# Feature attention with its mixing cut in two between heads, ten early maxima, and key casts one tile ahead

## The chip, the cores and the metric

The kernel runs on one core of a Trainium2 chip. Its engines run their own instruction queues in order and meet at semaphores: TensorE (PE: matmul, and PEld its weight load), VectorE (DVE), ScalarE (ACT), GpSimd (POOL), SyncE (SP, which issues the DMAs). The metric is the device time of one execution in microseconds (us), lower is better.

## The reference

A decoder of two layers over x (32 x 64 rows of 256) and a context of the same size, in fp32. Two of its six parts are touched: the first (differential attention) at its end, and the second, which is the feature attention below. It attends between the 256 *columns* of each batch, in 8 heads of 8 rows.

```
x = x + differential_attention(layernorm(x))
x = x + feature_attention(layernorm(x), ctx, ctx, W)

def feature_attention(q, k, v, W):            # q, k, v: (32, 64, 256)
    qh, kh, vh = (a.reshape(32, 8, 8, 256) for a in (q, k, v))
    a = einsum('bhdq,bhdk->bhqk', qh, kh) * 8 ** -0.5
    p = softmax(a, axis=-1)                    # 256 x 256 for each of 32 x 8
    y = einsum('bhqk,bhdk->bhdq', p, vh).reshape(32, 64, 256)
    return selu(einsum('oc,bct->bot', W, y))
```

## The kernel before

The 2048 rows are 16 tiles of 128 rows (two batches, b = 0 and 1). Queries and keys are split into bf16 parts and stacked in DRAM and back (`q_stack`, `k_stack`, lanes of 64 partitions), so that a bf16 matmul of 48 rows gives fp32 products.

The feature attention runs in *turns*, t = -1 to 16, and in turn t each engine works on several tiles. For every head h of every batch b of tile t+1, PE computes the scores (`largest`, L1015, two matmuls into PSUM bank h % 2) and DVE takes the row maximum (`maximum`, L842). So 16 maxima go through two banks, and PE may refill a bank only after DVE has read it (`max_taken`). Beside each `largest` PE computes the scores of tile t (`score`, L1020), with the maxima of the turn before as three further rows of the query stack. ACT turns each pair of heads into exponentials (`exponentials`, L901, 128 x 1024). `mix(tile, slot, b, half)` (L1032) multiplies the exponentials of four heads by the values, eight matmuls of 32 columns. These are the four *mixes* of a turn; I write "mix 0.1" for batch 0, half 1, and "head 0.3" for batch 0, head 3.

What follows a mix: ACT copies the result (`take_mixed`, L905, once for each batch), PE transposes it (`turn_mixed`, L1040), DVE divides by the sums (`divide`, L853 and L856), PE transposes both batches (L1093), ACT copies (`mixed_c`, L918), PE multiplies by W (`w_out`, L1101), ACT and POOL make the selu (L927 to L938, L998 to L1004) and add it to x.

How the maxima reach the queries: when 8 of them are taken, POOL splits them into three bf16 parts (`split_max`, four instructions, L980 to L986), PE transposes them (`turn_max`, L1047), ACT copies them (`max_to_rows`, L895) and SP writes them with two DMAs into the query stack (`max_to_stack`, L806). The heads of that batch in the next stage wait for the landing (`max_stacked`).

The order of the work is written out by hand for each engine. On PE a turn is eight calls `heads(b, g)`, each two heads with nothing between them, with the other work between these calls:

```
heads(0,0) mix(t-1) 1.1, turn_max(t,1)     heads(0,1) turn_mixed(t-1,1)
heads(0,2) transposes of mixed             heads(0,3) mix 0.0
heads(1,0) w_out                           heads(1,1) mix 0.1, turn_max(t+1,0)
heads(1,2) turn_mixed(t,0), context        heads(1,3) mix 1.0
```

The differential attention before it is also a pipeline in turns, t = -3 to 16, bound by PE except at its end. Turns 15 and 16 drain it: PE transposes probabilities (L629), multiplies by values (L672), transposes `scaled` (L683) and `headsT` (L690), multiplies by the output weights (L696); DVE sums squares (L553), scales (L563), divides and subtracts (L569 to L576) and adds to x (L579). Its last turns also carry the casts and splits of the context into `k_parts` (ACT L478, POOL L361 to L365).

## Time and profile before

| | us |
|---|---|
| median of 3 runs | 1336.93 |
| lowest, highest | 1335.71, 1339.19 |
| profiled execution, its own time | 1332.79 |
| its span from first to last instruction | 1330.7 |
| PE busy, DVE busy, ACT busy | 1215.3, 958.9, 709.2 |
| feature attention, about | 212 to 450 |

The profiled execution lies 4.1 us under the median. The timeline view gives, for each instruction or run of like instructions, its start, its length, the engine and line, what it writes and reads, how many, and in brackets how long the engine was idle before it and what released it.

### The profile page before, as it was taken

The numbers are of one execution on the slowest core, as the hardware profiler recorded it, in microseconds if no ns is written. First come the engines' busy times: TensorE is split into PE (matmuls) and PEld (weight loads), VectorE is DVE, ScalarE is ACT, GpSimd is POOL, SyncE is SP. The second block draws the span as 40 slices with busy tenths as digits, with TensorE's granted clock in tenths as the row PEclk, the third lists the DMA queues.
The fourth block names the chain that finished last, engine by engine and source line by source line (L and its number), as shares of the span: only waits on it lengthen the run. The fifth ranks groups of instructions, "written<-read, shape, count | busy, mean of one in ns | idle before, by whom it ended". The sixth has DMA issues, their size and how long they took to land. (4 is left out here: it accounts for less than half of the span.)

```text
span 1330.7 us, 27523 instructions
## 1 busy us (share of the span) xinstructions
PE 1215.3 (91%) x9976; PEld 963.9 (72%) x9976; DVE 958.9 (72%) x1862; ACT 709.2 (53%) x1475; POOL 454.5 (34%) x537
## 2 busy tenths in 40 slices
PE   4999988988888779798899999999997999999998
PEld 3677764444444557697677878788786899999998
DVE  5899986888887376887567778677775668555555
ACT  2778763777778546000466565656653463333332
POOL 1444642354553224565552423323240301112210
PEclk8999997999999988899999999999999999999999
DMA  5111161133231210000400000000000300000001
GB/s 173 36 36 37 46 147 32 41 80 95 77 94 35 55 60 0 1 0 13 135 9 4 4 8 4 8 4 8 4 1 9 87 25 25 25 25 25 1 1 64
DMA packets 58660, 51.04 MB, mean 38 GB/s; under 512 B 9064, under 2 KB 50888, under 8 KB 58184
## 3 DMA queue, kind: packets, MB, share of 16 engines
q1 hardware_dynamic: 58574, 49.88, 13.4%
q8 instruction: 56, 0.92, 0.3%
q14 instruction: 30, 0.25, 0.1%
HBM read 37.93 MB, written 11.53 MB: 37 GB/s over the span
## 5 line engine op out<-in xcount | busy, mean ns | idle before, releaser
L842 DVE TENSOR_REDUCE fa_neg_max<-psum 128x2 f32<-128x512 f32 x256 | 163.6, 685 | 35.6 <-PE psum L1015 34.7
L901 ACT ACTIVATE fa_probs<-psum 128x1024 f32<-128x1024 f32 x128 | 130.3, 1020 | 45.5 <-PE psum L1020 44.9
L1872 PE MATMUL psum<-mo_xT_high,mo_w_high 128*128 128x256 f32 x512 | 145.2, 284 | 3.0 <-DVE mo_xT_low L2706 2.8
L1872 PE MATMUL psum<-mo_xT_low,mo_w_high 128*128 128x256 f32 x512 | 144.9, 283 | 0.0
L1872 PE MATMUL psum<-mo_xT_high,mo_w_low 128*128 128x256 f32 x512 | 144.2, 282 | 0.0
L2538 ACT ACTIVATE mo_silu<-psum 128x256 f32<-128x256 f32 x128 | 49.0, 384 | 155.0 <-PE psum L1872 155.0
L2672 DVE TENSOR_TENSOR mo_mid<-mo_silu,psum 128x256 f32<-128x256 f32 x128 | 53.6, 419 | 92.8 <-ACT mo_silu L2538 92.7
L1015 PE MATMUL psum<-stacks_k_stack,stacks_q_stack 48*128 48x256 bf16 x512 | 93.5, 287 | 16.7 <-DVE fa_neg_max L842 7.7
L2008 POOL TENSOR_TENSOR ga_probs<-ga_probs,ga_top 128x1024 f32<-128x1024 f32 x16 | 30.5, 1905 | 203.6 <-DVE ga_top L2162 203.6
L1872 PEld LDWEIGHTS psum<-mo_xT_high,mo_w_high 128*128 128x128 f32 x512 | 97.0, 189 | 3.4 <-DVE mo_xT_low L2706 3.0
L1872 PEld LDWEIGHTS psum<-mo_xT_low,mo_w_high 128*128 128x128 f32 x512 | 97.2, 190 | 0.0
L1872 PEld LDWEIGHTS psum<-mo_xT_high,mo_w_low 128*128 128x128 f32 x512 | 97.0, 189 | 0.0
L2479 POOL TENSOR_TENSOR mo_w_low<-mo_raw,mo_w_high 128x512 fp32r<-128x512 f32 x21 | 27.6, 1315 | 188.0 <-ACT mo_w_high L2513 188.0
L1020 PE MATMUL psum<-stacks_q_stack,stacks_k_stack 51*128 51x256 bf16 x512 | 87.4, 280 | 0.2 <-DMA stacks_q_stack<-fa_max_rows 0.2
L1015 PEld LDWEIGHTS psum<-stacks_k_stack,stacks_q_stack 48*128 48x128 bf16 x512 | 33.0, 96 | 72.4 <-DVE fa_neg_max L842 42.2
L1997 POOL TENSOR_TENSOR ga_q_scaled<-ga_q,ga_q_inv 128x1024 f32<-128x1024 f32 x32 | 70.1, 2190 | 38.0 <-ACT ga_q_inv L2039 38.0
L2032 ACT ACTIVATE ga_q_scaled<-ga_q 128x512 f32<-128x512 f32 x64 | 40.3, 632 | 61.8 <-DVE ga_q L2135 61.8
L1032 PE MATMUL psum<-fa_probs,fa_values 128*32 128x256 f32 x1024 | 70.0, 392 | 2.5 <-ACT fa_probs L901 0.4
L1872 PE MATMUL psum<-mo_w_high,mo_mid_high 128*128 128x256 f32 x256 | 72.3, 282 | 0.0
L1872 PE MATMUL psum<-mo_w_low,mo_mid_high 128*128 128x256 f32 x256 | 71.9, 281 | 0.0
L1872 PE MATMUL psum<-mo_w_high,mo_mid_low 128*128 128x256 f32 x256 | 71.7, 280 | 0.0
L2335 PE MATMUL psum<-ga_w_o_high,ga_mixedT_high 128*128 128x256 f32 x256 | 63.0, 287 | 4.9 <-DVE ga_mixedT_low L2154 4.9
(434 smaller groups left out, 3548.0 us busy)
## 6 DMA issues: line engine op xcount, KB each, us to landing
k_parts<-da_k_parts SPq DMA_DIRECT2D x96, 64.0 KB, 2.0
stacks_k_stack<-k_parts SPq DMA_DIRECT2D x32, 192.0 KB
q_parts<-stacks_parts SPq DMA_DIRECT2D x48, 64.0 KB, 2.0
stacks_q_stack<-q_parts SPq DMA_DIRECT2D x32, 96.0 KB
x<-in_x SPq DMA_DIRECT2D x4, 512.0 KB, 7.7
da_context<-in_ctx SPq DMA_DIRECT2D x4, 512.0 KB, 7.9
stacks_q_stack<-q_parts SPq DMA_DIRECT2D x32, 64.0 KB
fa_context<-in_ctx SPq DMA_DIRECT2D x16, 128.0 KB, 2.2
```

What stands on the lines that cost most here:

```text
L842: nc.vector.tensor_reduce(neg_max[:, b, :, head_at(h)], ps[:, h % 2, :].rearrange("p (q k) -> p q k", q=2), AX.X, ALU.max, negate=True).th ...
L901: nc.scalar.activation(probs[:, g].rearrange("p h k q -> p h (k q)"), ps[:, 2 + 2 * (g % 2):4 + 2 * (g % 2), :], ACT.Exp).then_inc(exp_don ...
L1015: return nc.tensor.matmul(ps[:, h % 2, q * E:(q + 1) * E], q_stack[lane, slot, b, h // LANES, q * P:(q + 1) * P], k_stack[lane, slot, b, h ...
L1020: return nc.tensor.matmul(ps[:, 2 + h % 4, k * E:(k + 1) * E], k_stack[lane, slot, b, h // LANES, k * P:(k + 1) * P], q_stack[lane, slot, ...
L1032: done = nc.tensor.matmul(ps[32 * c:32 * c + 32, 6, half * E:(half + 1) * E], values[:, slot, k, 8 * b + head_at(h), :], probs[:, h // 2, ...
L1872: done = nc.tensor.matmul(out, lhsT[i], rhs[j], start=start and k == 0, stop=stop and k == 2)
L1997: nc.gpsimd.tensor_tensor(q_scaled[:, columns].rearrange("p (h d) -> p h d", d=G_HD), q[:, columns].rearrange("p (h d) -> p h d", d=G_HD), ...
L2008: nc.gpsimd.tensor_tensor(probs[:], probs[:], top[:, :, None].to_broadcast([P, G_HEADS, SEQ]), ALU.subtract).then_inc(shifted, 1)
L2032: nc.scalar.activation(q_scaled[:, g * G_CHUNK:(g + 1) * G_CHUNK], q[:, g * G_CHUNK:(g + 1) * G_CHUNK], ACT.Square).then_inc(squares_ready, 1)
L2335: nc.tensor.matmul(ps[:, 6, 0:E], mixedT_high[:, h], weight[:, h], start=(h == 0 and weight is w_o_high), stop=False)
L2538: nc.scalar.activation(silu[:, j % 4], ps[:, j % 4, 0:2 * P], ACT.Silu).then_inc(silu_ready, 1)
L2672: nc.vector.tensor_tensor(mid[:, j % 4], silu[:, j % 4], ps[:, j % 4, 2 * P:4 * P], ALU.mult).then_inc(mid_ready, 1)
```

## The change

Four things are changed.

1. **Mixing in halves.** `mix` gets an argument k and issues only four of its eight matmuls. Each half stands after a single head: `heads(b, g)` becomes `head(b, h)`. The first half waits as the mix did, the second waits for nothing, and `mixed_done` comes with the second. Around it, `w_out` moves from after `heads(1,0)` to after head 1.3 and also waits for `max_rows_ready` of the next tile; `turn_max(t+1, 0)` no longer waits for `channels_read`; `divide(t-1, 1)` moves two heads later on DVE.
2. **ACT and POOL orders.** `take_mixed(t, 0)` and `max_to_rows(t+1, 0)` stand ahead of `exponentials(t, 1, 1)`. POOL adds the selu one turn later, and splits the maxima ahead of the queries and of clearing the values.
3. **Ten early maxima.** Of tile 0's 16 maxima, ten are scored and taken in turns 15 and 16 of the differential attention, through banks 4 and 5. The stack of tile 0 gets a semaphore of its own.
4. **Key casts.** ACT casts the context of tile t+2 instead of tile t+1 in a turn; the last split waits for `values_ready`.

```diff
+    def take_maximum(self, core, bank, b, h):
+        return core.nc.vector.tensor_reduce(self.neg_max[:, b, :, head_at(h)], core.psum[:, bank, :].rearrange("p (q k) -> p q k", q=2),
+                                            AX.X, ALU.max, negate=True)
...
+                stacks.load_q(sp, n, n, stacked if n else first_stacked)
+                stacks.load_k(sp, n, n, stacked if n else first_stacked)
...
+                    if valid(t) and not valid(t + 2):
+                        pool.wait_ge(values_ready, t + 1)
                     split_keys(t + 1)
...
+                if at(t, -1):
+                    act.wait_ge(context_loaded[0], 16)
                     nc.scalar.copy(k_parts[:, t + 1, 0], context[:, t + 1]).then_inc(k_highs, 1)
+                    for group in context_loaded[1:]:
+                        act.wait_ge(group, 16)
+                if started(t, -1) and valid(t + 2):
+                    nc.scalar.copy(k_parts[:, t + 2, 0], context[:, t + 2]).then_inc(k_highs, 1)
...
+            def early_maxima(first, last):
+                for n in range(first, last):
+                    dve.wait_ge(early_scored, n + 1)
+                    stacks.take_maximum(core, 4 + n % 2, n // C_HEADS, n % C_HEADS).then_inc(early_taken, 1)
...
+                if at(t, TILES - 1):
+                    early_maxima(0, 3)
+                if at(t, TILES):
+                    early_maxima(6, 7)
...
+                if at(t, TILES - 1):
+                    early_maxima(3, 6)
+                if at(t, TILES):
+                    early_maxima(7, EARLY_MAXIMA)
...
+            def early_scores(first, last):
+                if first == 0:
+                    pe.wait_ge(first_stacked, 16 * (LANES + LANES * PARTS))
+                    pe.wait_ge(shifted[1], TILES)
+                    pe.wait_ge(ones_loaded, 16 * LANES)
+                for n in range(first, last):
+                    if n >= 2:
+                        pe.wait_ge(early_taken, n - 1)
+                    for q in range(2):
+                        done = stacks.largest(core, 4 + n % 2, 0, n // C_HEADS, n % C_HEADS, q)
+                    done.then_inc(early_scored, 1)
...
+                if at(t, TILES - 1):
+                    early_scores(0, 2)
...
+                if at(t, TILES - 1):
+                    early_scores(2, 4)
...
                     if at(t, TILES):
+                        early_scores(6, 8)
...
+                if at(t, TILES):
+                    early_scores(8, EARLY_MAXIMA)
...
+                if at(t, TILES - 1):
+                    early_scores(4, 6)
...
+            dve.sem_inc(max_taken, EARLY_MAXIMA)
+
             def maximum(tile, b, h):
+                if isinstance(tile, int) and 16 * tile + 8 * b + h < EARLY_MAXIMA:
+                    return
                 dve.wait_ge(max_scored, 16 * tile + (8 * b + h + 1))
-                nc.vector.tensor_reduce(neg_max[:, b, :, head_at(h)], ps[:, h % 2, :].rearrange("p (q k) -> p q k", q=2),
-                                        AX.X, ALU.max, negate=True).then_inc(max_taken, 1)
+                stacks.take_maximum(core, h % 2, b, h).then_inc(max_taken, 1)
...
-                        if g == 1 and b == 0 and valid(t - 1):
+                        if g == 2 and b == 0 and valid(t - 1):
                             divide(t - 1, 1)
-                        if g == 2 and b == 0 and valid(t - 2):
+                        if g == 0 and b == 1 and valid(t - 2):
                             row_stats(t - 2)
                         if g == 2 and b == 1 and valid(t):
                             divide(t, 0)
...
                     exponentials(t, 0, 3)
-                if valid(t):
                     exponentials(t, 1, 0)
+                    take_mixed(t, 0)
+                if valid(t + 1):
+                    max_to_rows(t + 1, 0)
+                if valid(t):
+                    exponentials(t, 1, 1)
                 if valid(t - 1):
                     act.wait_ge(projected, t)
                     if started(t, 2):
                         act.wait_ge(selu_sum, t - 1)
                     nc.scalar.activation(below[:], ps[:, 7, E:2 * E], ACT.Relu, scale=-1.0).then_inc(selu_parts, 1)
                     nc.scalar.activation(above[:], ps[:, 7, E:2 * E], ACT.Relu, scale=SELU_SCALE).then_inc(channels_read, 1)
...
             def turn(t, ring, rounds, valid):
+                if isinstance(t, int) and t == -1:
+                    pool.sem_inc(split_done, 1)
+                if valid(t - 2):
+                    add_selu(t - 2)
+                if valid(t + 1):
+                    split_max(t + 1, 0)
+                if isinstance(t, int) and t == -1:
+                    clear_values()
                 if valid(t + 3) and started(t, 1):
                     split(t + 3, ring(3), rounds(3))
-                if isinstance(t, int) and t == -1:
-                    pool.sem_inc(split_done, 1)
-                    clear_values()
...
                 if valid(t + 1):
                     split_max(t + 1, 1)
+                if isinstance(t, int) and t == TILES:
+                    add_selu(t - 1)
...
-            def mix(tile, slot, b, half):
-                pe.wait_ge(exp_done, 8 * tile + (4 * b + 2 * half + 2))
-                if half == 0:
-                    if b or started(tile, 1):
-                        pe.wait_ge(mixed_ready, 2 * tile + b)
-                    pe.wait_ge(values_ready, tile + 1)
-                for k in range(2):
-                    for c in range(4):
-                        h = 4 * half + c
-                        done = nc.tensor.matmul(ps[32 * c:32 * c + 32, 6, half * E:(half + 1) * E], values[:, slot, k, 8 * b + head_at(h), :],
-                                                probs[:, h // 2, h % 2, k, :], start=(k == 0), stop=(k == 1), skip_group_check=True)
-                done.then_inc(mixed_done, 1)
+            def mix(tile, slot, b, half, k):
+                if k == 0:
+                    pe.wait_ge(exp_done, 8 * tile + (4 * b + 2 * half + 2))
+                    if half == 0:
+                        if b or started(tile, 1):
+                            pe.wait_ge(mixed_ready, 2 * tile + b)
+                        pe.wait_ge(values_ready, tile + 1)
+                for c in range(4):
+                    h = 4 * half + c
+                    done = nc.tensor.matmul(ps[32 * c:32 * c + 32, 6, half * E:(half + 1) * E], values[:, slot, k, 8 * b + head_at(h), :],
+                                            probs[:, h // 2, h % 2, k, :], start=(k == 0), stop=(k == 1), skip_group_check=True)
+                if k == 1:
+                    done.then_inc(mixed_done, 1)
 
...
+                def head(b, h):
...
-                heads(0, 0)
+                head(0, 0)
                 if valid(t - 1):
-                    mix(t - 1, ring(-1), 1, 1)
+                    mix(t - 1, ring(-1), 1, 0, 1)
+                head(0, 1)
+                if valid(t - 1):
+                    mix(t - 1, ring(-1), 1, 1, 0)
+                head(0, 2)
+                if valid(t - 1):
+                    mix(t - 1, ring(-1), 1, 1, 1)
                 if valid(t):
                     pe.wait_ge(values_ready, t + 1)
                     turn_max(t, 1)
...
-                heads(0, 3)
-                if valid(t):
-                    mix(t, ring(0), 0, 0)
-                heads(1, 0)
-                if valid(t - 1):
-                    pe.wait_ge(mixed_c_ready, t)
-                    nc.tensor.matmul(ps[:, 7, E:2 * E], w_out[:], mixed_c[:], start=True, stop=True).then_inc(projected, 1)
-                heads(1, 1)
-                if valid(t):
-                    mix(t, ring(0), 0, 1)
+                head(0, 7)
+                if valid(t):
+                    mix(t, ring(0), 0, 0, 0)
+                head(1, 0)
+                if valid(t):
+                    mix(t, ring(0), 0, 0, 1)
+                head(1, 1)
                 if valid(t + 1):
                     if isinstance(t, int) and t == -1:
                         pe.wait_ge(loaded, 32)
                     if valid(t - 1):
-                        pe.wait_ge(channels_read, t)
+                        pe.wait_ge(mixed_c_ready, t)
                     elif valid(t):
                         pe.wait_ge(max_rows_ready, 2 * t + 2)
                     turn_max(t + 1, 0)
-                heads(1, 2)
+                if valid(t):
+                    mix(t, ring(0), 0, 1, 0)
+                head(1, 2)
+                if valid(t):
+                    mix(t, ring(0), 0, 1, 1)
+                head(1, 3)
+                if valid(t - 1):
+                    pe.wait_ge(mixed_c_ready, t)
+                    if valid(t + 1):
+                        pe.wait_ge(max_rows_ready, 2 * t + 3)
+                    nc.tensor.matmul(ps[:, 7, E:2 * E], w_out[:], mixed_c[:], start=True, stop=True).then_inc(projected, 1)
+                head(1, 4)
                 if valid(t):
                     turn_mixed(t, 0)
+                head(1, 5)
+                head(1, 6)
...
+                    if valid(t - 1):
+                        pe.wait_ge(channels_read, t)
...
-                heads(1, 3)
-                if valid(t):
-                    mix(t, ring(0), 1, 0)
+                head(1, 7)
+                if valid(t):
+                    mix(t, ring(0), 1, 0, 0)
```

What now stands in a row on PE in a steady turn of the feature attention, from the middle of batch 0's heads to the middle of batch 1's. L1015 and L1020 (before), L204 and L1074 (after) are `largest` and `score`, L1032 and L1086 the mixing, L1101 and L1182 `w_out`, L1047 and L1102 `turn_max`; "..." stands for further rows of heads alone. Before:

```order
L1093 MATMUL psum<-ident,fa_mixed 128x128 x2
...
L1032 MATMUL psum<-fa_probs,fa_values 32x256 x8
L1015 MATMUL psum<-stacks_k_stack,stacks_q_stack 128x256
L1020 MATMUL psum<-stacks_q_stack,stacks_k_stack 128x256
...
L1101 MATMUL psum<-fa_mixed_c,fa_w_out 128x256
...
L1032 MATMUL psum<-fa_probs,fa_values 32x256 x8
L1047 MATMUL psum<-fa_ident_bf,fa_max_parts 24x128 x2
```

After:

```order
L1155 MATMUL psum<-ident,fa_mixed 128x128 x2
...
L1086 MATMUL psum<-fa_probs,fa_values 32x256 x4
L204 MATMUL psum<-stacks_k_stack,stacks_q_stack 128x256
L1074 MATMUL psum<-stacks_q_stack,stacks_k_stack 128x256
...
L1102 MATMUL psum<-fa_ident_bf,fa_max_parts 24x128 x2
L1086 MATMUL psum<-fa_probs,fa_values 32x256 x4
...
L1182 MATMUL psum<-fa_mixed_c,fa_w_out 128x256
```

Each block of eight is now two blocks of four with one head between them, `turn_max` stands ahead of both halves of mix 0.1 and `w_out` behind them.

ACT in the same turn, from the copy `mixed_c` (L918, after L971) on; L901 and L954 are the exponentials, L905 and L958 `take_mixed`, L895 and L948 `max_to_rows`, L927/L928 and L984/L985 the two selu parts. Before:

```order
L918 COPY fa_mixed_c<-psum 128x256
L901 ACTIVATE fa_probs<-psum 128x1024 x2
L927 ACTIVATE fa_below<-psum 128x256
L928 ACTIVATE fa_above<-psum 128x256
L901 ACTIVATE fa_probs<-psum 128x1024
L905 COPY fa_mixedT<-psum 128x512
L895 CAST fa_max_rows<-psum 24x256
L938 ACTIVATE fa_exp_below<-fa_below 128x256
```

After:

```order
L971 COPY fa_mixed_c<-psum 128x256
L954 ACTIVATE fa_probs<-psum 128x1024 x2
L958 COPY fa_mixedT<-psum 128x512
L948 CAST fa_max_rows<-psum 24x256
L954 ACTIVATE fa_probs<-psum 128x1024
L984 ACTIVATE fa_below<-psum 128x256
L985 ACTIVATE fa_above<-psum 128x256
L989 ACTIVATE fa_exp_below<-fa_below 128x256
```

The copy and the cast moved ahead of one exponential and of the selu parts, which follow `w_out`.

DVE in turn 15 of the differential attention and the start of turn 16. Before:

```order
L553 TENSOR_REDUCE da_square_sum<-da_squares 128x16
L563 TENSOR_TENSOR da_scaled<-da_attn,da_rms_inv 128x256
L569 RECIPROCAL da_inv<-psum 128x32
L571 TENSOR_TENSOR da_part<-psum,da_inv 128x256
```

After:

```order
L573 TENSOR_REDUCE da_square_sum<-da_squares 128x16
L208 TENSOR_REDUCE stacks_neg_max<-psum 128x2 x3
L587 TENSOR_TENSOR da_scaled<-da_attn,da_rms_inv 128x256
L208 TENSOR_REDUCE stacks_neg_max<-psum 128x2 x3
L597 RECIPROCAL da_inv<-psum 128x32
L599 TENSOR_TENSOR da_part<-psum,da_inv 128x256
```

Three maxima (L208) stand ahead of `scaled` and three ahead of the reciprocal. PE at the same place, before:

```order
L672 MATMUL psum<-da_probsT,da_values 64x2x64 x16
L683 MATMUL psum<-ident,da_scaled 128x128 x2
L690 MATMUL psum<-ident,da_headsT 128x128 x8
L696 MATMUL psum<-da_w_o,da_attnT 128x256 x2
```

After:

```order
L715 MATMUL psum<-da_probsT,da_values 64x2x64 x16
L204 MATMUL psum<-stacks_k_stack,stacks_q_stack 128x256 x4
L729 MATMUL psum<-ident,da_scaled 128x128 x2
L738 MATMUL psum<-ident,da_headsT 128x128 x8
L204 MATMUL psum<-stacks_k_stack,stacks_q_stack 128x256 x4
L746 MATMUL psum<-da_w_o,da_attnT 128x256 x2
```

The scores of maxima 2 and 3 stand behind the product with the values, those of 4 and 5 behind the transposes of `headsT`; those of 0 and 1 stand further up.

## Rows read from the trace of the kernel before

**Rows 1.** Windows of the whole core, us: start:end length, engines, clock, DMA share

```profile
200.00:206.00 6.00, 5.72 (x63) 5.13 (x62) 2.26 (x6) 3.15 (x8) 0.61 (x2) 1.00 0.26 66
...
216.00:222.00 6.00, 5.43 (x20) 1.14 (x18) 5.59 (x11) 0.36 (x1) 1.42 (x6) 0.50 0.01 2
...
340.00:360.00 20.00, 17.92 (x216) 8.23 (x218) 17.17 (x33) 15.75 (x25) 8.95 (x22) 1.00 0.38 98
```

**Rows 2.** Group of instructions, 212 to 440 us: busy, mean ns, idle before

```profile
L842 DVE TENSOR_REDUCE fa_neg_max<-psum 128x2 f32<-128x512 f32 x256 | 163.6, 685 | 35.6 <-PE psum L1015 34.7
```

**Rows 3.** Timeline, one steady turn: start, length, instruction, idle before it

```profile
267.95 0.27 PE L1015 MATMUL psum<-stacks_k_stack,stacks_q_stack 48*128 48x256 bf16 x1 [0.44 <-DMA stacks_q_stack<-fa_max_rows]
...
268.37 1.29 DVE L842 TENSOR_REDUCE fa_neg_max<-psum 128x2 f32<-128x512 f32 x2 [0.82 <-PE psum L1015]
...
272.11 0.41 PE L1093 MATMUL psum<-ident,fa_mixed 128*128 128x128 f32 x2 [0.18 <-DVE fa_mixed L856]
...
273.21 0.28 PE L1015 MATMUL psum<-stacks_k_stack,stacks_q_stack 48*128 48x256 bf16 x1 [0.20 <-DVE fa_neg_max L842]
...
273.54 1.07 PE L1032 MATMUL psum<-fa_probs,fa_values 128*32 128x256 f32 x16
...
274.54 0.28 PE L1015 MATMUL psum<-stacks_k_stack,stacks_q_stack 48*128 48x256 bf16 x1
...
274.75 0.22 POOL L980 TENSOR_TENSOR fa_max_parts<-fa_neg_max,stacks_zeros 128x16 bf16<-128x16 f32 x1 [1.68 <-DVE fa_neg_max L842]
...
274.96 2.48 DVE L842 TENSOR_REDUCE fa_neg_max<-psum 128x2 f32<-128x512 f32 x4 [0.29 <-PE psum L1015]
...
275.08 0.70 PE L1101 MATMUL psum<-fa_mixed_c,fa_w_out 128*128 128x256 f32 x2
...
275.65 0.22 POOL L986 TENSOR_TENSOR fa_max_parts<-fa_max_rest,fa_max_parts 128x16 bf16<-128x16 f32 x1
...
276.63 1.07 PE L1032 MATMUL psum<-fa_probs,fa_values 128*32 128x256 f32 x16
...
277.52 0.28 PE L1047 MATMUL psum<-fa_ident_bf,fa_max_parts 128*24 128x128 bf16 x2
...
277.77 0.59 ACT L905 COPY fa_mixedT<-psum 128x512 f32<-128x512 f32 x1
...
278.16 1.29 DVE L842 TENSOR_REDUCE fa_neg_max<-psum 128x2 f32<-128x512 f32 x2 [0.71 <-PE psum L1015]
278.25 0.36 ACT L895 CAST fa_max_rows<-psum 24x256 bf16<-24x256 f32 x1
```

**Rows 4.** Timeline of DVE and PE: starts of turn 1 and turn 15

```profile
240.92 0.28 PE L1015 MATMUL psum<-stacks_k_stack,stacks_q_stack 48*128 48x256 bf16 x1
...
431.61 0.40 PE L1020 MATMUL psum<-stacks_q_stack,stacks_k_stack 51*128 51x256 bf16 x4 [0.19 <-DMA stacks_q_stack<-fa_max_rows]
```

**Rows 5.** Timeline, last two turns of the differential attention

```profile
200.76 1.97 PE L672 MATMUL psum<-da_probsT,da_values 128*64 128x128 f32 x32 [0.28 <-POOL da_values L388]
...
201.63 0.42 DVE L563 TENSOR_TENSOR da_scaled<-da_attn,da_rms_inv 128x256 f32<-128x256 f32 x1 [2.18 <-ACT da_rms_inv L451]
...
204.10 0.36 DVE L569 RECIPROCAL da_inv<-psum 128x32 f32<-128x32 f32 x1 [2.04 <-PE psum L690]
...
210.50 0.43 DVE L581 BATCH_NORM_STATS2 row_stats<-x 128x6 f32<-128x256 f32 x1
```

**Rows 6.** Timeline, start of the feature attention

```profile
213.73 8.26 DVE L842 TENSOR_REDUCE fa_neg_max<-psum 128x2 f32<-128x512 f32 x12 [1.17 <-PE psum L1015]
...
225.01 0.37 PE L1015 MATMUL psum<-stacks_k_stack,stacks_q_stack 48*128 48x256 bf16 x1 [0.37 <-DMA stacks_q_stack<-fa_max_rows]
```

**Rows 7.** Page, DMA issues: count, KB each, us from issue to landing

```profile
fa_context<-in_ctx SPq DMA_DIRECT2D x16, 128.0 KB, 2.2
```

**Rows 8.** Timeline, last turns of the feature attention

```profile
437.08 0.40 PE L1020 MATMUL psum<-stacks_q_stack,stacks_k_stack 51*128 51x256 bf16 x4
...
441.92 1.93 PE L1032 MATMUL psum<-fa_probs,fa_values 128*32 128x256 f32 x32 [0.39 <-ACT fa_probs L901]
```

96 lines of the change are left out of this document (44 added, 52 removed).

## The prediction

> **What bounds the kernel now.** I read the windows first: the feature attention runs at the full clock from about 238 us on, with PE busy 17.92 and DVE 17.17 of 20 us, so neither engine has much to spare and neither is full [rows 1]. The groups then say what DVE waits for: its 256 maxima take 163.6 us and it stands idle 35.6 us before them, nearly all on PE's scores [rows 2]. The timeline says where. Turn 1 starts at 240.92 and turn 15 at 431.61 [rows 4], so 14 steady turns take 190.7 us, 13.62 each. In one such turn [rows 3] DVE idles 0.82 us at the start, 0.29 after mix 0.0 and 0.71 after mix 0.1 with `turn_max`. The first of these is no mixing: PE's head 0.0 waits there 0.44 us for the DMA that carries the maxima. So two loops hold a turn at 13.6 us, the two PSUM banks between PE and DVE, and a chain mix 0.1, `take_mixed`, `max_to_rows`, DMA, head 0.0 of the next turn. The change touches both. What to see in these rows: the 16 matmul instructions of mix 0.0 cost DVE only 0.29 us as they stand.
>
> **The prices for a steady turn**, all from [rows 3], clock 1.00:
> - A maximum follows the last after 0.60 us (four in 2.48) and lasts 0.68. DVE starts 0.42 after PE starts a head (274.54 to 274.96), and PE starts the head two further on about 0.06 after the maximum that frees its bank.
> - The second head of a pair to the mix: 273.21 to 273.54, 0.33. A mix to the next head: 273.54 to 274.54, 1.00. To `turn_max` it is 0.89. Two mixes in a row, in turn 16, take 1.93 against 1.07 for one [rows 8], so eight matmuls take 0.86 and 0.14 is lost once for each block. Half a mix then is 0.43 + 0.14 = 0.57 to the next head.
> - A head alone, with no other kind behind it, is 0.23. So a head with half a mix is 0.33 + 0.57 = 0.90 on PE, against 0.60 on DVE.
> - `take_mixed` starts 1.14 after its mix (276.63 to 277.77), so 0.71 after a last half; the cast for the rows ends 0.84 later (278.61). The four POOL instructions of `split_max` take 1.12 (274.75 to 275.87). From the rows (278.61) to the head that needs them, the next head 0.0 at 267.95 + 13.6 = 281.55, it is 2.95.
>
> **Mixing in halves.** PE's own work rises. Four more blocks are entered and left, at 0.10 (0.33 less 0.23) and 0.14: 1.0 us a turn. Before the change an estimate by these prices for all of PE's blocks is 11 us of 13.6, and 12 after, of a turn that I now walk. Times are from PE's start of head 0.0.
> Half mix, 0.1 at 0.90, half mix, 0.2 at 1.80, half mix and `turn_max(t,1)` at 2.6, 0.3 at 2.8, 0.4 at 3.0. The copy of batch 1 can start only 0.71 after its last half, at 2.8, so `turn_mixed` comes at 3.5 and 0.5 at 4.0. Head 0.6 waits for an exponential and a bank until 4.7. DVE divides after head 0.5, to 5.6, and the transposes of `mixed` start at 5.75 (before at 272.11, which is 4.16). Head 0.7 at 6.1, half mix, 1.0 at 7.0, half mix, 1.1 at 7.9. Before, 1.0 stands at 6.6. Then a stall: maximum 0.7 ends at 7.2, POOL has split it at 8.35, and `turn_max(t+1,0)`, which came 2.8 us after the POOL start, now stands at 8.2 and waits to 8.5. Half of mix 0.1, 1.2 at 9.3, second half at 9.6, 1.3 at 10.2. `take_mixed` starts at 10.3 and the rows are there at 11.15 (before at 10.66, which is 278.61). **The new wait:** `w_out` now needs these rows. PE is through with head 1.3 at 10.5 and stands 0.7 us to 11.25; behind it in PE's queue is every head of the rest of the turn, and DVE waits for them. Head 1.4 comes at 11.8 (before 9.8), `turn_mixed` at 12.1, 1.5 at 12.6. DVE takes maximum 1.5 from 13.0 to 13.7 and divides to 14.2, so 1.7 is on PE at 13.8, the last half mix at 14.3 and the next head 0.0 at 14.9, where the bank is free too. The DMA landed at 14.15 and is no longer the last. The same walk with the old order gives every start of [rows 3] to within some 0.1 us and 13.6 for the turn, which is why I trust it.
> The walk gives 14.9 us, 1.3 more a turn. Two prices no row shows. The second half waits for no semaphore, so the way into it may be short of 0.33: bounded by 0.22 (back to back with the head's 0.23) and 0.33. And a half might lose less than 0.14 (at least 0: 0.43) or more (at most the fill of a whole block, 0.64). With the low ends throughout, 0.25 + 0.43, the walk still gives 14.1, because the POOL stall grows and the wait for the rows stays; with the high ones 15.4. I take the upper middle, 14.8, nearest to the rows measured: +1.2 x 14 = **+16.8 us** (+7 to +25).
> Here a rule of the skill bears on the price. [Rows 3] show 0.10 into and 0.14 out of a block of mixing, between heads on 64-row lanes and a mix on 32-column strips. The Trainium skill, page "TensorEngine Tiling (Array Packing)", section "Key Properties", says that changing the tiling mode, not just the tile, drains the engine; by that rule four more blocks pay both ends, as summed above, and without it the low end (14.1) would hold.
>
> **Last turns.** Turn 15 has no maxima. PE's first halves again stand ahead of `turn_max(15,1)`: rows at 3.6 and head 1.0 at 6.6 after its start, where the profile has 437.08 less 431.61, 5.5 [rows 4, 8]. From head 1.0 on the copy for batch 0 now stands ahead of exponential 1.1 and the selu parts ahead of 1.2, so the last exponential ends some 1.4 later than now. Together **+2.5** (bounds +1 and +3).
>
> **Turn 0** runs at half clock before and, I take it, after. The same walk with doubled PE prices gives 15.3 us against 15.9 (225.01 to 240.92 [rows 4, 6]): **-0.6** (-2 to +1).
>
> **Early maxima, in the drain** [rows 5]. Maxima 0 and 1 fit behind `square_sum` while DVE waits 2.18 us for the root. But DVE's queue has maximum 2 ahead of `scaled`, and its score stands on PE behind the product with the values, which starts at 200.76 and ends at 202.7. DVE gets it at 203.1 and `scaled` comes at 203.7 instead of 201.63. Its transposes and those of `headsT` behind them are late by 1.5. Then maxima 4 and 5, scored behind these transposes at 205.4, run to 207.1, and the reciprocal starts at 207.0 instead of 204.10: 2.9 late. All after it is a chain (attn, squares, root, scaled, output, x); maximum 6 hides in the wait for the root, 7 to 9 behind the last transposes. The end, 210.93, is **+3.0** later (+2 to +3.5).
>
> **Early maxima, at the start of the feature attention** [rows 6]. Twelve maxima run 213.73 to 221.99 and the last of 16 ends at 225.4, PE's turn 0 starting at 225.01. After the change only six are left. They stand behind `turn_max(0,0)`, which now waits for two small loads issued at 212.4 and 212.8 (landing some 2.2 later [rows 7]), so the first starts near 215.95 on the same scale. Two maxima, 0.8 us of statistics, and four more at 0.69, with the context's transposes between the last two, end at 221.0; PE starts turn 0 at 220.4. That is **-4.6** (-6.5, if the loads are quicker, to -3).
>
> **Key casts.** ACT's cast, POOL's split of keys 15 and then the values' copy held PE 0.28 us at 200.76 [rows 5]; ACT's copy of the probabilities is ready only 0.1 before that. **-0.1** (-0.3 to +0.2). The rest of that attention is bound by PE. POOL's work is the same, only earlier.
>
> **Sum**: 16.8 + 2.5 - 0.6 + 3.0 - 4.6 - 0.1 = +17.0 us. On the profiled execution's own 1332.79 us that is 1349.8. The median of the runs lies 4.1 above it, and I put the same change on that: 1336.93 + 17.0 = 1354.
>
> **Rivals.**
> 1. *The drain of a half is cheap* (0.25 + 0.43): turns of 14.1, +7 in place of +16.8, sum +7.2, 1344. For it: the second halves wait for nothing. Against: 0.14 is lost at each block seen. Chance 0.2.
> 2. *Halves close DVE's gaps as they are placed to*, and the kernel is faster. Mechanism: if head plus half a mix fits in DVE's 0.60 us, DVE runs through from 0.0 to 1.3, and each turn loses its idle of 0.82 + 0.29 + 0.71 less the 0.7 at `w_out`: 12.5 us, -1.1 x 14 = -15.4, and with the other parts about -15, 1322. It decides at 0.60 on PE for a head with half; the rows say 0.90, and two bf16 pairs with eight passes of mixing alone are 0.23 + 0.43 = 0.66. If only half of this comes, some -5. Chance 0.1.
> 3. *No change to measure*: turns of 13.7, the early maxima's net -1.6 paying for them. It needs both low prices and `w_out` not waiting, as if mix 0.1 ended a head earlier. Chance 0.05.
> 4. *The early maxima cost more than they give*: the clock falls earlier in the longer drain or turn 0 runs at half clock throughout, +3 to +5 on top of my sum, 1358. At 216 to 222 us the granted clock is 0.50, the 1.2 GHz level, with PE waiting for DVE [rows 1]; after, PE has still less to do there. Chance 0.1.
> My own forecast has 0.55.
>
> **Chances and range.** Faster by over 0.3% (4 us, about what a measurement of this kernel can tell from no change) 0.1, within 0.05, slower 0.85. The range of 1340 to 1362 takes in rival 1, rival 4 and the bounds of the half's price; it leaves out rivals 2 and 3.
>
> **What would show it.** In the profile after: turns of 14.8 us; DVE idle 0.3 us before nearly every maximum beside a half mix, and some 0.9 after head 1.3; PE waiting 0.7 us ahead of L1182 for the cast of the rows; no more wait for the DMA at head 0.0; heads with a half between them 0.90 apart. In the drain the reciprocal of turn 15 starts 2.9 later, and 4.6 are won before turn 0. I am wrong if heads with a half between follow each other in 0.7 us or less, or if `w_out` finds the rows ready.

## The result: 1.2% slower

The changed kernel takes 1351.11 us in the median of 4 runs (1347.38 to 1355.31), the kernel before 1336.32 in the median of its 4. The ratio is 1.0124, 95% interval 1.0099 to 1.0150, so 13 to 20 us are lost, 14.8 by the medians. Forecast were 1354 and +17.

The profiled execution of after has a span of 1353.1 us, 22.4 more than that of before. It is the slowest of its four, and that of before lies below the median of its own, so the two traces lie 7.6 us further apart than the medians. The windows of the whole core, as in [rows 1] (stretch, length, busy time and count of PE, PEld, DVE, ACT, POOL, granted clock, DMA share, GB/s), with a steady stretch of the feature attention last:

```profile
216.00:222.00 6.00, 4.25 (x20) 1.34 (x20) 4.22 (x13) 1.12 (x4) 2.91 (x2) 0.50 0.26 82
...
280.00:300.00 20.00, 17.34 (x204) 6.61 (x206) 16.52 (x31) 14.37 (x22) 9.50 (x23) 1.00 0.31 75
```

and the group of the maxima, from the page, as in [rows 2] (busy time, mean ns of one, idle time before them and who ended most of it):

```profile
L208 DVE TENSOR_REDUCE stacks_neg_max<-psum 128x2 f32<-128x512 f32 x256 | 172.5, 689 | 52.0 <-PE psum L204 50.6
```

DVE now stands 52.0 us ahead of its maxima where it stood 35.6 (the new group also counts the ten early ones), and in a steady stretch PE and DVE are both less busy than they were: 17.34 and 16.52 us in 20, against 17.92 and 17.17. More waits, then, not only more work. Over the 14 steady turns PE was busy 12.07 us a turn before and 12.88 after; the idle rest went from 1.55 to 2.21. One steady turn shows them. The columns are start, length, instruction, and in brackets the idle time before it and who ended it. L208 is the maximum, L1074 `score` (the rows shown are each the first of a head), L1086 half a mixing block, L1102 the turning of maxima, L1155 the transposes of `mixed`, L1182 the product with `w_out`:

```profile
281.61 0.28 PE L1074 MATMUL psum<-stacks_q_stack,stacks_k_stack 51*128 51x256 bf16 x1
...
281.93 0.64 PE L1086 MATMUL psum<-fa_probs,fa_values 128*32 128x256 f32 x8
282.50 0.28 PE L1074 MATMUL psum<-stacks_q_stack,stacks_k_stack 51*128 51x256 bf16 x1
282.82 0.64 PE L1086 MATMUL psum<-fa_probs,fa_values 128*32 128x256 f32 x8
...
283.40 0.28 PE L1074 MATMUL psum<-stacks_q_stack,stacks_k_stack 51*128 51x256 bf16 x1
...
285.06 0.66 PE L1095 MATMUL psum<-ident,fa_mixedT 128*128 128x128 f32 x4
...
287.40 0.41 PE L1155 MATMUL psum<-ident,fa_mixed 128*128 128x128 f32 x2 [0.69 <-DVE fa_mixed L909]
...
290.21 0.22 PE L1102 MATMUL psum<-fa_ident_bf,fa_max_parts 128*24 128x128 bf16 x1 [0.28 <-POOL fa_max_parts L1037]
...
291.87 0.58 ACT L958 COPY fa_mixedT<-psum 128x512 f32<-128x512 f32 x1 [0.85 <-PE psum L1086]
...
292.35 0.36 ACT L948 CAST fa_max_rows<-psum 24x256 bf16<-24x256 f32 x1
...
292.86 0.67 PE L1182 MATMUL psum<-fa_mixed_c,fa_w_out 128*128 128x256 f32 x2 [0.73 <-ACT fa_max_rows L948]
...
296.83 0.28 PE L1074 MATMUL psum<-stacks_q_stack,stacks_k_stack 51*128 51x256 bf16 x1
```

Head 0.0 starts at 281.61, and the first three heads follow each other with half a block between them by 0.89 (282.50, 283.40). PE waits 0.69 us for DVE's division and 0.73 at the product with `w_out` for the cast of the rows at 292.35. (Between 300 and 400 us these two waits are 0.79 and 0.63 a turn.) The maxima are turned at 290.21. The next head 0.0 comes at 296.83, 15.2 us after the last. Over all, turn 1 starts at 236.42 and turn 15 at 447.68, 14 turns of 15.09 where [rows 4] gave 13.62:

```profile
236.42 0.28 PE L1074 MATMUL psum<-stacks_q_stack,stacks_k_stack 51*128 51x256 bf16 x1
...
447.68 0.39 PE L1074 MATMUL psum<-stacks_q_stack,stacks_k_stack 51*128 51x256 bf16 x2
```

**The bill, piece by piece**, each from the same instruction in both traces:

| Stretch | Before | After | Difference | Forecast |
|---|---|---|---|---|
| up to the first tile's addition to x | 52.41 | 51.25 | -1.2 | none |
| from there to tile 13's addition (key casts) | 145.85 | 145.32 | -0.5 | -0.1 |
| drain, to the last addition | 11.78 | 14.74 | +3.0 | +3.0 |
| to the first head of turn 0 | 14.97 | 10.14 | -4.8 | -4.6 |
| turn 0 | 15.91 | 14.97 | -0.9 | -0.6 |
| 14 steady turns | 190.69 | 211.26 | +20.6 | +16.8 |
| turn 15 to the last statistics of x | 19.95 | 22.20 | +2.2 | +2.5 |
| all behind the feature attention | 879.1 | 883.2 | +4.1 | none |

The last line lies in code that the change leaves alone, and so does most of the first, which moves by itself: over the twelve kernels below it stood between 50.1 and 54.4. Without both, the change costs 19.5 us in this pair of executions; the medians say 14.8, and the interval of the ratio ends at 20.

### The profile page after: what moved, and what is told of

It reads as the page before. It is cut to its first block and busy times, and to the rows that moved or that the text cites. A ratio compares the mean times of both kernels' runs of the same rounds, so it can differ in the third digit from the quotient of the medians.

```text
span 1353.1 us, 27548 instructions
## 1 busy us (share of the span) xinstructions
PE 1233.3 (91%) x9976; PEld 958.8 (71%) x9976; DVE 971.2 (72%) x1862; ACT 710.8 (53%) x1475; POOL 453.9 (34%) x537
## 5 line engine op out<-in xcount | busy, mean ns | idle before, releaser
L208 DVE TENSOR_REDUCE stacks_neg_max<-psum 128x2 f32<-128x512 f32 x256 | 172.5, 689 | 52.0 <-PE psum L204 50.6
L954 ACT ACTIVATE fa_probs<-psum 128x1024 f32<-128x1024 f32 x128 | 129.8, 1023 | 37.2 <-PE psum L1074 37.2
L204 PE MATMUL psum<-stacks_k_stack,stacks_q_stack 48*128 48x256 bf16 x512 | 97.8, 282 | 8.5 <-ACT fa_probs L954 3.3
L2082 POOL TENSOR_TENSOR ga_probs<-ga_probs,ga_top 128x1024 f32<-128x1024 f32 x16 | 30.5, 1905 | 203.7 <-DVE ga_top L2236 203.7
L1074 PE MATMUL psum<-stacks_q_stack,stacks_k_stack 51*128 51x256 bf16 x512 | 98.1, 279 | 0.3 <-ACT fa_probs L954 0.2
L204 PEld LDWEIGHTS psum<-stacks_k_stack,stacks_q_stack 48*128 48x128 bf16 x512 | 28.4, 95 | 84.8 <-issue 47.6
L1086 PE MATMUL psum<-fa_probs,fa_values 128*32 128x256 f32 x1024 | 83.1, 396 | 2.8 <-ACT fa_probs L954 0.7
```

The source lines that it names most:

```text
L204: return core.nc.tensor.matmul(core.psum[:, bank, q * E:(q + 1) * E], self.q_stack[lane, slot, b, h // LANES, q * P:(q + 1) * P], self.k_s ...
L208: return core.nc.vector.tensor_reduce(self.neg_max[:, b, :, head_at(h)], core.psum[:, bank, :].rearrange("p (q k) -> p q k", q=2), AX.X, A ...
L954: nc.scalar.activation(probs[:, g].rearrange("p h k q -> p h (k q)"), ps[:, 2 + 2 * (g % 2):4 + 2 * (g % 2), :], ACT.Exp).then_inc(exp_don ...
L1074: return nc.tensor.matmul(ps[:, 2 + h % 4, k * E:(k + 1) * E], k_stack[lane, slot, b, h // LANES, k * P:(k + 1) * P], q_stack[lane, slot, ...
L1086: done = nc.tensor.matmul(ps[32 * c:32 * c + 32, 6, half * E:(half + 1) * E], values[:, slot, k, 8 * b + head_at(h), :], probs[:, h // 2, ...
L2082: nc.gpsimd.tensor_tensor(probs[:], probs[:], top[:, :, None].to_broadcast([P, G_HEADS, SEQ]), ALU.subtract).then_inc(shifted, 1)
```

## The experiments

Each kernel was timed beside the kernel before on the same chip, but not all on one chip: "halves joined" to "halves, old order" shared one, the next four a second, the next three a third, and the last had a fourth. Ratios of different groups are compared through the kernel before. "Turn" is the mean steady turn of the profiled execution, from the cast of the rows in turn 1 to that in turn 15.

| Kernel | Ratio to before (95%) | Turn, us |
|---|---|---|
| before | 1 | 13.62 |
| after | 1.0124 (1.0099 to 1.0150) | 15.09 |
| halves joined | 1.0243 (1.0207 to 1.0278) | 15.81 |
| `w_out` later | 1.0066 (1.0042 to 1.0090) | 14.28 |
| early maxima and casts alone | 0.9976 (0.9956 to 0.9996) | 13.58 |
| halves, old order | 1.0050 (1.0019 to 1.0082) | 14.06 |
| new order, whole blocks | 1.0092 (1.0075 to 1.0109) | 14.60 |
| early maxima placed anew | 0.9944 (0.9927 to 0.9961) | 13.59 |
| two exchanges | 0.9998 (0.9972 to 1.0025) | 13.73 |
| exchanges, maxima and casts | 0.9977 (0.9964 to 0.9991) | 13.69 |
| exchanges and POOL's order | 0.9940 (0.9916 to 0.9963) | 12.98 |
| all of these | 0.9895 (0.9839 to 0.9951) | 13.00 |
| all of these, in halves | 1.0062 (1.0038 to 1.0086) | 14.30 |
| all of these, one block divided | 0.9881 (0.9856 to 0.9907) | 12.82 |

### Which part costs what: dividing, or the order

**Early maxima and casts alone.** The feature attention's orders are those of before; only the drain, the first turn and the casts are as changed.

> The changed kernel with the feature attention's old order (whole mixing blocks, w_out between heads 1.1 and 1.2, ACT, DVE and POOL as before), so the early maxima and the earlier key casts alone. From the two traces: 2.9 us lost in the drain, 4.4 won before turn 0, 0.5 from the casts, turns of 13.6 as before. Sum -2.0 us, ratio 0.9985; the drain's reciprocal again 2.9 us late. The rival, that the early maxima also hurt or help turn 0 by its clock, would show turn 0 more than 1 us off 15.9 and the sum beyond -1 to -3.

Measured: 0.9976, -3.2 us. The drain took 2.9 more than before (tile 13's addition to x at 199.60, tile 14's at 209.96), the stretch of the casts 0.5 less, and from the end of the drain to the first rows of turn 1 it was 5.4 us less. Start and turn 0 together thus gave 5.4, where I had put 4.4 for the start and nothing for turn 0. The start alone gave 5.6 here (the first head of turn 0 comes 9.40 after the last addition, 14.97 before, 10.14 in the changed kernel). The part as a whole is a small gain, and its loss in the drain is real.

**Halves in the old order.** Each second half stands where the whole block stood, each first half one head earlier:

```diff
+                if valid(t):
+                    mix(t, ring(0), 0, 0, 0)
                 head(0, 7)
                 if valid(t):
-                    mix(t, ring(0), 0, 0, 0)
                     mix(t, ring(0), 0, 0, 1)
                 head(1, 0)
                 head(1, 1)
...
```

This is one block of the four; the other three are divided in the same way.

> The early maxima and casts as changed, and the mixing in halves, but each second half where the whole block stood before and each first half one head earlier, with w_out, the turning of the maxima and the orders of ACT, DVE and POOL as before. Against the kernel with early maxima and casts alone it shows what dividing costs by itself. My theory: four more blocks at 0.24 are 1.0 us of PE; heads with a half between follow at 0.90 instead of 0.60 for DVE; turns of 14.4 (14.2 to 14.7). If the new order of w_out, ACT and POOL is worth something to the halves, as the change supposes, this one is above 15.1; if dividing is free, it stays at 13.6.

Measured: turns of 14.06, below the low end of my range. Dividing by itself costs 14.06 - 13.58 = 0.48 us a turn, half of the 1.0 that I had summed for PE. PE's busy time rose by 0.36 of that (12.06 to 12.42 a turn), the rest is idle time.

**The new order with whole blocks.** It is the counterpart, in short form against the kernel with early maxima and casts alone (ACT's and POOL's orders are those of the changed kernel, too; DVE's, with `divide(t-1, 1)` where it was, is that of before):

```diff
 head(1, 0); head(1, 1)
-w_out product
+turn_max(t + 1, 0)
 head(1, 2); head(1, 3)
 mix(t, ring(0), 0, 1, 0); mix(t, ring(0), 0, 1, 1)
-turn_max(t + 1, 0)
+pe.wait_ge(max_rows_ready, 2 * t + 3)
+w_out product
 head(1, 4)
```

> The counterpart of the kernel with halves in the old order: whole mixing blocks between pairs of heads, as before, with the changed place of the product with w_out (behind head 1.3 and mix 0.1, waiting for the rows of the maxima), the changed place of the turning of the maxima (ahead of head 1.2) and the changed orders of ACT and POOL; early maxima and key casts as changed. By the first runs dividing costs 0.5 us a turn and the order 1.0. If the order costs by itself, w_out waits here some 1.1 us for the rows, since mix 0.1 ends just ahead of it, and the turn is 14.6 us or more. The rival, that the order costs only together with halves (because their last one ends late), expects turns of 13.6 to 13.9.

Measured: 14.60, so the order by itself costs 1.02. The two shares, 0.48 and 1.02, add up to 1.50, and the changed kernel is 1.51 above the kernel with early maxima and casts alone. That the sum fits so well doesn't prove that these are the changed kernel's own shares: its halves stand in other places than those of the kernel with 0.48, and it has a later division on DVE too. The list of waits (300 to 400 us, in total, times, longest) of this kernel names the two new ones, 0.96 us a turn for the rows at L1177, which is `w_out` here, and 0.77 for POOL's split:

```profile
PE psum L1177 <- ACT fa_max_rows L948: 6.7, 7, 1.0
PE psum L1102 <- POOL fa_max_parts L1037: 5.4, 7, 0.8
```

One part of the order was run by no kernel alone, DVE's later `divide(t-1, 1)`. The longest of PE's waits in the changed kernel's list is for it, at the transposes of `mixed`:

```profile
PE psum L1155 <- DVE fa_mixed L909: 5.5, 7, 0.9
```

With whole blocks and DVE's old order the same wait is

```profile
PE psum L1151 <- DVE fa_mixed L909: 1.3, 7, 0.2
```

How much of the first comes from the later place of the division, and how much from the later end of batch 1's last half, is open.

**The product with `w_out` one place later**, all else as changed:

```diff
+                head(1, 4)
+                if valid(t):
+                    turn_mixed(t, 0)
                 if valid(t - 1):
                     pe.wait_ge(mixed_c_ready, t)
                     ...
-                head(1, 4)
-                if valid(t):
-                    turn_mixed(t, 0)
```

> The changed kernel with the product with w_out one place later: behind head 1.4 and the transposes of the mixed rows of batch 0, instead of ahead of head 1.4. PE stood 0.73 us before it for the cast of the rows, with head 1.4 and all later heads behind it. My theory: the wait is on the path of the turn; head 1.4 comes some 1.4 us earlier and head 1.5 some 0.8, and the turn falls by 0.7 to 14.4 us, some 10 us in all. The rival: a later wait (the DMA of the maxima, or the context's transposes, which need the channels read) takes its place and the turn stays within 0.2 us of 15.1.

Measured: 14.28, -0.81 a turn, and 1.0066 instead of 1.0124. So the wait for the rows was on the path, and in the profiled turns more than half of what the turn had lost is undone by moving one product past one head. A new wait for the channels (the context's transposes at L1194) is there, but short of what went:

```profile
PE psum L1182 <- ACT fa_max_rows L948: 4.4, 7, 0.6
```

```profile
PE psum L1194 <- ACT fa_above L985: 2.1, 7, 0.3
```

The first line is of the changed kernel, the second of this one.

### Is it the number of blocks? A theory that fell

My prediction priced a block by its way in and out, 0.24 us, and summed four of them. Taking these four away again should then give back most of 1.0 us.

```diff
                 head(0, 0)
                 if valid(t - 1):
+                    mix(t - 1, ring(-1), 1, 0, 0)
                     mix(t - 1, ring(-1), 1, 0, 1)
                 head(0, 1)
-                if valid(t - 1):
-                    mix(t - 1, ring(-1), 1, 1, 0)
                 head(0, 2)
                 if valid(t - 1):
+                    mix(t - 1, ring(-1), 1, 1, 0)
                     mix(t - 1, ring(-1), 1, 1, 1)
...
```

> The changed kernel, in which the two halves of each mixing block stand together again, where the second one stood; all else is as changed. PE enters and leaves four blocks fewer in a turn. My theory (a block costs 0.24 us beyond its matmuls, 0.10 going in and 0.14 coming out) takes 1.0 us off PE in each turn of 15.1, of which a part is lost again at the waits that stay (the product with w_out waits for the rows of the maxima): turns of 14.3 us, 14.1 to 14.6, some 11 us less than the changed kernel and 0.7% above the kernel before. The rival, that dividing costs next to nothing and the new order of the rest costs it all, expects turns of 15.0.

Measured: 1.0243 and turns of 15.81. With four blocks fewer the kernel is another 1% slower. Neither theory had this. The timeline (PE, DVE, ACT) shows what a turn loses there:

```profile
329.88 1.07 PE L1086 MATMUL psum<-fa_probs,fa_values 128*32 128x256 f32 x16
331.31 0.69 DVE L208 TENSOR_REDUCE stacks_neg_max<-psum 128x2 f32<-128x512 f32 x1 [0.64 <-PE psum L204]
331.43 1.07 PE L1086 MATMUL psum<-fa_probs,fa_values 128*32 128x256 f32 x16
331.43 1.02 ACT L954 ACTIVATE fa_probs<-psum 128x1024 f32<-128x1024 f32 x1 [1.63 <-PE psum L1074]
```

The whole block stands between the two heads of a pair. An exponential (L954) takes both heads of a pair, so ACT waits 1.63 us for the second one, and DVE, with one of its two banks served, 0.64. What PE saves at the blocks' ends it gives back as a torn pair. In four of the 14 turns (16.6 to 16.8 us, the others 14.3 to 15.8 and 15.5 in the mean) a stretch at a lower granted clock comes on top:

```profile
334.00:336.00 2.00, 0.97 (x12) 0.34 (x11) 1.74 (x5) 1.35 (x2) 0.11 (x1) 1.00 0.02 6
336.00:338.00 2.00, 2.00 (x18) 0.89 (x22) 1.45 (x3) 1.40 (x2) 0.22 (x1) 0.55 0.86 223
```

The granted 0.55, near the 1.2 GHz level, follows a stretch of 2 us in which PE was busy for 0.97. That stretch is not what sets the four turns apart, for a like one stands in each of the other ten, where the clock stays at 1.00:

```profile
270.30:272.30 2.00, 0.92 (x12) 0.34 (x11) 1.76 (x5) 1.33 (x2) 0.10 (x1) 1.00 0.02 6
```

Why the clock fell in four turns and not in the others is open. So this run doesn't measure the price of a block alone, as I had meant it to. It shows that, as placed here, fewer blocks are no gain. The ten turns without the lower clock, 15.5 in the mean, are still 0.4 longer than the changed kernel's.

### The drain and the start

The trace of after, for the drain: the score of maximum 2 is in the queue behind the product with the values (L715), DVE waits 2.44 us for it ahead of `scaled`, and maxima 4 and 5 run ahead of the reciprocal:

```profile
196.57 0.41 DVE L607 TENSOR_TENSOR x<-x,psum 128x256 f32<-128x256 f32 x1
...
199.07 1.97 PE L715 MATMUL psum<-da_probsT,da_values 128*64 128x128 f32 x32 [0.28 <-issue]
...
201.40 0.69 DVE L208 TENSOR_REDUCE stacks_neg_max<-psum 128x2 f32<-128x512 f32 x1 [2.44 <-PE psum L204]
202.01 0.41 DVE L587 TENSOR_TENSOR da_scaled<-da_attn,da_rms_inv 128x256 f32<-128x256 f32 x1
...
204.15 1.29 DVE L208 TENSOR_REDUCE stacks_neg_max<-psum 128x2 f32<-128x512 f32 x2 [1.12 <-PE psum L204]
205.35 0.35 DVE L597 RECIPROCAL da_inv<-psum 128x32 f32<-128x32 f32 x1
...
206.93 0.41 DVE L607 TENSOR_TENSOR x<-x,psum 128x256 f32<-128x256 f32 x1
```

```diff
-EARLY_MAXIMA = 10
+EARLY_MAXIMA = 9
...
                 if at(t, TILES - 1):
-                    early_maxima(3, 6)
+                    early_maxima(3, 5)
...
                 if valid(t):
                     turn_probs(1)
+                if at(t, TILES - 1):
+                    early_scores(2, 3)
...
                 if at(t, TILES - 1):
-                    early_scores(2, 4)
+                    early_scores(3, 5)
...
-                if at(t, TILES - 1):
-                    early_scores(4, 6)
...
-                if valid(t + 1):
+                if valid(t + 1) and not (isinstance(t, int) and t == -1):
                     ...
                     turn_max(t + 1, 0)
                 head(1, 4)
                 head(1, 5)
+                if isinstance(t, int) and t == -1:
+                    pe.wait_ge(loaded, 32)
+                    turn_max(0, 0)
```

> The early maxima placed anew, with the feature attention's old order: nine instead of ten, maximum 2 scored ahead of the product with the values, maxima 3 and 4 behind it and ahead of the transposes of the scaled rows, and at the start of the feature attention the turning of the first maxima (which waits for two loads) behind heads 1.4 and 1.5. If the drain lost its 2.9 us because the score of maximum 2 and those of 4 and 5 stood behind work of PE's that DVE's queue then waited for, the loss falls to 0.5, and DVE's maxima start some 2.5 us earlier after the switch: 6.5 won there instead of 4.4. Together with the casts -6.5 us against the kernel before, ratio 0.995. The rival, that any maximum in the drain costs its 0.65 us of DVE, keeps 2.5 to 3 of loss there.

Measured: 0.9944, -7.5 us. From tile 13's addition (198.70) to tile 14's (206.36) it is 7.66 us, against 7.42 before and 10.36 after: 0.2 lost instead of 2.9, with five of the nine maxima in it (the whole drain takes 12.04, against 11.78 and 14.74). That refutes the rival: five maxima in turn 15 cost nothing like 0.65 each, it was the place of their scores. Where the five lie:

```profile
199.81 1.28 DVE L208 TENSOR_REDUCE stacks_neg_max<-psum 128x2 f32<-128x512 f32 x2
...
201.27 0.69 DVE L208 TENSOR_REDUCE stacks_neg_max<-psum 128x2 f32<-128x512 f32 x1 [0.19 <-PE psum L204]
202.07 0.43 DVE L587 TENSOR_TENSOR da_scaled<-da_attn,da_rms_inv 128x256 f32<-128x256 f32 x1
203.53 1.29 DVE L208 TENSOR_REDUCE stacks_neg_max<-psum 128x2 f32<-128x512 f32 x2 [1.02 <-PE psum L204]
204.77 0.36 DVE L597 RECIPROCAL da_inv<-psum 128x32 f32<-128x32 f32 x1
```

Maxima 0 and 1 are the first row, 2 the second, 3 and 4 the fourth.

At the start of the feature attention DVE's first maxima come at 214.59 in place of 217.13. Counted from the last addition of the drain (210.74 and 211.31) that is 3.85 us and 5.82, so 2.0 earlier, since PE no longer waits there for `fa_w_out` to land first. After:

```profile
216.17 0.39 PE L1102 MATMUL psum<-fa_ident_bf,fa_max_parts 128*24 128x128 bf16 x2 [1.36 <-DMA fa_w_out<-in_fa_w_out]
...
217.13 1.29 DVE L208 TENSOR_REDUCE stacks_neg_max<-psum 128x2 f32<-128x512 f32 x2 [3.29 <-PE psum L204]
```

and the kernel with the maxima placed anew:

```profile
214.59 1.89 DVE L208 TENSOR_REDUCE stacks_neg_max<-psum 128x2 f32<-128x512 f32 x3 [1.32 <-PE psum L204]
```

But turn 0 does not start earlier for it: its first head comes 10.2 us after the last addition, where it came 9.4 to 10.1 in the six kernels with ten early maxima. So of the 4.3 us between this kernel and that with early maxima and casts alone (0.9944 and 0.9976) the drain explains 2.7 and the start nothing that shows; I had expected 2 more won there. In the profiled execution the way from that head to the first rows of turn 1 was 1.7 us shorter as well, at a granted clock of 0.71 in the first 15 us of turn 0 against 0.55. The later kernel with "all of these" has the same start, a clock of 0.54 and no such gain.

The two pieces of this edit, in the drain and at the start, were not run apart; what each gave is read from the trace.

### What holds a turn at 13.6

**Two exchanges**, on the kernel before:

```diff
                 if valid(t):
                     exponentials(t, 1, 1)
-                    take_mixed(t, 0)
                 if valid(t + 1):
                     max_to_rows(t + 1, 0)
+                if valid(t):
+                    take_mixed(t, 0)
...
-                if valid(t):
-                    turn_mixed(t, 0)
                 if valid(t + 1):
                     pe.wait_ge(context_ready[ring(1)], 16 * rounds(1) + 16)
                     ...
                     done.then_inc(values_psum, 1)
+                if valid(t):
+                    turn_mixed(t, 0)
```

> The kernel before with two exchanges alone: ACT casts the rows of the maxima before it copies the mixed rows, and PE transposes the context before the mixed rows. In the turn before, PE's head 0.0 waited 0.44 us for the DMA that carries these rows. If that DMA is one of the two things that hold a turn at 13.6, the rows leave 0.45 us earlier and the turn falls to 13.2, -5.6 us in all. The rival: the banks between PE and DVE hold the turn alone and it stays within 0.1 of 13.6.

Measured: 0.9998, turns of 13.73. The waits for the DMA at head 0.0 are gone from the list, and one that [rows 3] did not have is in it, 4.8 us in 100:

```profile
PE psum L1015 <- DMA stacks_q_stack<-fa_max_rows: 2.2, 7, 0.3
```

```profile
PE psum L1048 <- POOL fa_max_parts L987: 4.8, 8, 0.8
```

Here the first line is of the kernel before, the second of this one, and L1048 the turning of the maxima of batch 1. That is what took the DMA's place. In the kernel before POOL's split was ready just in time, at 269.40, and PE turned the maxima at 269.55:

```profile
269.18 0.22 POOL L986 TENSOR_TENSOR fa_max_parts<-fa_max_rest,fa_max_parts 128x16 bf16<-128x16 f32 x1
269.55 0.27 PE L1047 MATMUL psum<-fa_ident_bf,fa_max_parts 128*24 128x128 bf16 x2
```

So the rival, that the turn stays, came true (it is 0.1 longer, if anything), though not for the reason it gave, as the next run shows.

**And POOL's order.** The split of the maxima of batch 1 goes ahead of POOL's addition to x (0.72 us):

```diff
+                if valid(t + 1):
+                    split_max(t + 1, 1)
                 if valid(t - 1):
                     pool.wait_ge(selu_sum, t)
                     nc.gpsimd.tensor_tensor(core.x[:, t - 1, :], core.x[:, t - 1, :], selu[:], ALU.add).then_inc(x_ready, 1)
-                if valid(t + 1):
-                    split_max(t + 1, 1)
```

> The kernel with the two exchanges (rows of the maxima cast first, context transposed first) and one more: POOL splits the maxima of batch 1 of the next tile ahead of its addition to x, not behind it. With the exchanges alone PE no longer waited for the DMA at head 0.0 but 0.55 to 0.85 us at the turning of the next maxima for POOL's split, which stood behind the addition (0.73 us), and the turn stayed at 13.7. My theory: with that gone too the turn falls to 13.0 to 13.2, -7 us against the kernel before. The rival, that the two banks hold the turn and PE's waits are only where the time is shown, keeps it at 13.6.

Measured: 0.9940, turns of 12.98, just below the 13.0 to 13.2 that I expected. The first edit brings nothing alone, since POOL's split stood right behind the wait that it took away. Whether POOL's order alone would do it was not tried.

**Together.** The exchanges with the early maxima placed anew and the casts, without and with POOL's order:

> Both of the last two edits on the kernel before, with the earlier key casts: whole mixing blocks, early maxima placed anew, rows of the maxima cast first. If both hold, their gains add: -12 us, ratio 0.991. If the exchange brings nothing, -6.5.

> The same three edits of order in the feature attention together with the early maxima placed anew and the earlier key casts. If the turn falls to 13.1: 6.5 + 7, -13 us against the kernel before, ratio 0.990. If the turn stays, -6.5, ratio 0.995.

Measured: 0.9977 and 0.9895. The first adds nothing to the early maxima: it is 0.3% slower than without the exchanges (0.9944, and the intervals do not overlap), of which the turn of 13.69 in place of 13.59 explains 1.4 us in some 4; the rest is open. The second has both gains.

### Halves once more, with both waits gone

> The last kernel with the mixing in halves, placed as in the kernel with halves in the old order. If dividing costs PE 0.24 us for each of four more blocks, and PE is what holds the turn once both waits are gone, it is slower than the last kernel by 0.5 to 1.0 us a turn, +7 to +14 us. The rival, that halves pay once nothing but DVE's idle time before the maxima is left, expects it at or below the last kernel.

Measured: 1.0062, turns of 14.30 against 13.00. Dividing costs 1.30 here, more than my upper end, where it cost 0.48 in the old order. PE's busy time grew by 0.60 a turn (11.96 to 12.56) and its idle time by 0.70. The timeline shows where such idle time arises:

```profile
348.82 0.69 DVE L208 TENSOR_REDUCE stacks_neg_max<-psum 128x2 f32<-128x512 f32 x1 [0.50 <-PE psum L204]
348.86 1.02 ACT L954 ACTIVATE fa_probs<-psum 128x1024 f32<-128x1024 f32 x1 [0.99 <-PE psum L1078]
...
349.93 0.64 PE L1090 MATMUL psum<-fa_probs,fa_values 128*32 128x256 f32 x8 [0.25 <-ACT fa_probs L954]
```

With a half inside the pair ACT waits 0.99 us for the pair's second head, its exponential ends later, and the next half block, which reads it, waits 0.25 in turn. Between 300 and 400 us ACT's waits ahead of its exponentials grow from 18.0 to 24.9 us by the division (in the old order from 20.4 to 23.6). Why the same division cost 0.8 us a turn more here than in the old order was not taken apart.

**One block divided, and no pair torn.** Batch 0's first block: one half ahead of head 0.6, the other where the whole stood, behind head 0.7:

```diff
+                if valid(t):
+                    mix(t, ring(0), 0, 0, 0)
                 head(0, 6)
                 head(0, 7)
                 if valid(t):
-                    mix(t, ring(0), 0, 0, 0)
                     mix(t, ring(0), 0, 0, 1)
```

> The fastest kernel so far (whole blocks, turns of 13.0) with one block of the four divided, that of batch 0's first half, and both halves between pairs of heads: the first ahead of head 0.6, the second where the whole block stood. No pair of heads is torn. If a divided block costs what its matmuls' way in and out costs, the turn grows by 0.24 at most and falls short of that where DVE's wait behind the block (0.3) closes: 12.9 to 13.25, in all -1 to +3.5 us. If the price of halves is mostly that they stand between the two heads of a pair, the turn stays at 13.0 within 0.1. The rival, that any divided block costs a quarter of the 1.3 us that four cost there, expects 13.3.

Measured: 0.9881, turns of 12.82, 0.18 shorter than with whole blocks and outside both expectations on the good side. One block more, and a shorter turn (12.8 in 11 of the 14, against 13.0 in 12 of the 14). DVE waited 10.1 us in 100 for its scores, now 7.9:

```profile
DVE stacks_neg_max L208 <- PE psum L204: 10.1, 24, 0.7
```

```profile
DVE stacks_neg_max L208 <- PE psum L204: 7.9, 25, 0.4
```

Of the eight halves of the last kernel but one, and of the changed one, four stand within a pair of heads and four between pairs. The run with one block says that this half, between pairs, cost nothing and gained a little. That the four within carry the whole price of dividing fits this but is not shown: no run divided all four blocks without tearing a pair, and none divided one block inside a pair. The intervals of these last two ratios (0.9895 and 0.9881, from two chips) overlap; the difference of 0.18 a turn is read from one profiled execution of each. By their medians both are over 1% faster than the kernel before and over 2% faster than the changed one.

## Why the prediction was right, and where it was not

**The total.** Forecast +17, measured +14.8 by the medians and +19.5 by the pieces of the two traces. That it came out so near proves no term by itself; the terms are taken one by one here.

**What bounds the kernel.** Right in kind: PE, DVE and the chain of the maxima are all near the bound, and neither engine is full. The "two loops" that I named were one too few. With the DMA's wait gone, PE waited for POOL's split, which [rows 3] don't show as a wait because it was just in time there. PE's own work was set too low: PE is busy 12.07 us of a turn before, not 11, and the 17.92 in 20 of [rows 1] already come to 12.2.

**The steady turn.** The walk's starts, from head 0.0 on, agree with the measured ones: `turn_mixed` 3.5 and 3.5, the transposes of `mixed` 5.75 and 5.8, `turn_max(t+1,0)` 8.5 and 8.6, the rows 11.15 (ready) and 11.1, `w_out` 11.25 and 11.25, next head 0.0 14.9 and 15.2 in this turn, 15.09 in the mean. A head with half a block took 0.89 (forecast 0.90), and PE's wait for the rows 0.73 (forecast 0.7). DVE stood idle 1.03 us after head 1.3 (forecast 0.9), and the wait for the DMA at head 0.0 is gone. The step that was off is the last: having walked to 14.9, I took 14.8 because a cheaper entry into a second half could be. It was not cheaper (0.32 from the head, against 0.33), and the tail of the turn took more than walked, 0.2 in the mean and 0.3 in this one, where the half behind head 1.7 and the head after it each waited for an exponential. That is +20.6 instead of +16.8, inside the bounds I gave (+7 to +25).

**Where the time of the turn comes from.** Here the working was right in sum but would have led astray in a repair. I put 1.0 us on PE's four more blocks and saw the wait for the rows beside it. PE's busy time rose by 0.81 a turn, its idle time by 0.66. The runs give the order 1.02 (with halves in it, moving `w_out` undid 0.81) and dividing 0.48, in the orders of before. And a block's way in and out is no price that one can multiply: four fewer made it worse, one more made it better.

**The price of a half.** In after the second half of mix 1.0, which waits for no semaphore, starts 0.32 behind its head (281.61 to 281.93, priced 0.33), and the next head follows 0.57 later (282.50, priced 0.57); the first half behind it has 0.32 and 0.58. Rival 1, which needed 0.25 and 0.43, is out. The rule that the prediction cites from the Trainium skill (page "TensorEngine Tiling (Array Packing)", section "Key Properties"), that a change of the tiling mode drains the engine, agrees with this size. But no run took such a drain away by itself, so that it is the cause is not shown.

**Early maxima.** The drain's +3.0 was measured as +3.0 (2.94 of it up to tile 14's addition), and by the road that I gave. All of it stands 1.69 earlier in this execution, the product with the values at 199.07 in place of 200.76. With that added back, maximum 2 comes at 203.09 (forecast 203.1), `scaled` at 203.70 (203.7) and the reciprocal at 207.04 (207.0). The kernel with the maxima placed anew confirms the mechanism. The start gave 4.8 for 4.6, turn 0 0.9 for 0.6. Rival 4 (the clock stays lower for longer) did not come true: turn 0 had a granted clock of 0.65,

```profile
221.50:236.50 15.00, 13.61 (x117) 3.96 (x115) 11.38 (x20) 9.66 (x15) 1.76 (x8) 0.65 0.02 5
```

and over the same turn the kernel before has 0.59 (225 to 241 us). Over the first 15 us of turn 0 the kernels here have between 0.53 and 0.76, so the 0.9 can be the clock's as well as the change's.

**Key casts.** The bill says -0.5, but that depends on the mark it starts from. Between the first tile's addition and tile 13's the eleven kernels with early casts took 145.3 to 145.4 us, the three without 145.9, 146.1 and 147.4. Counted from PE's first product with the values (37.15 before, 35.61 after) to tile 13's addition, it is 161.12 us before and 160.96 after, -0.16; the eleven have 160.9 to 161.1, the three 161.1, 161.3 and 162.7. So the size, -0.1, holds, but not my reason: PE's 0.28 us ahead of the last product is still there at 199.07, put down to issue and no longer to POOL.

**Last turns.** +2.2 for +2.5, as walked: head 1.0 comes 6.4 after the start of turn 15 (forecast 6.6, before 5.5).

**Rivals 2 and 3.** Rival 2 asked for a head with half a block in 0.60, rival 3 for the low prices (0.25 + 0.43 = 0.68) and no wait at `w_out`. At 0.89 and 0.73 both were far off. The direction of rival 2 holds for one block placed between pairs, which I had not considered.

## What to carry to other kernels

Before a large block is divided to fill gaps, look at what its neighbours form together: here an exponential takes two heads, and a block or half between these two made ACT and DVE wait, while the one half that was placed between pairs was a small gain. When a product is moved behind a cast, everything behind it in PE's queue moves with it; ask who waits for that queue, and try it one place later. And where the removal of a wait brings nothing, look at once for the next wait in the same place, since two edits, of which the first was worth nothing alone and the second was not tried alone, were worth 0.6 us a turn together.

## What was not expected of the hardware

From 250 to 425 us all other kernels here run at a granted clock of 1.00 throughout, even the slowest turns of 15.1. The one with joined halves falls to 0.50 for over 3 us in four of its turns and then comes back; these four are the longest, 16.7 us in the mean against 15.5. What PE did just before does not tell them from the other ten: each turn of this kernel has a stretch of 2 us in which PE is busy for 1.04 us or less, and so has each turn of the changed kernel and of the one with the new order and whole blocks, where the clock never fell. The cause is open. For a reader the use is that a mean over turns can hide a few of another kind, so the turns should be looked at one by one before their mean is explained.
